# The last of 39 expert tiles added to the sums by one-hot matmuls in PSUM instead of by a scatter, and the final layer norm read from PSUM

## The reference

```
x = _layernorm(x + attn(x, ...), axis=-1)
x = _layernorm(x + xattn(x, ctx, ctx, W, b), axis=-1)
x = _layernorm(x + ffn(x, Wg, bg, W1, b1, W2, b2), axis=-1)      # the change is in this line

def ffn(x, Wg, bg, W1, b1, W2, b2):
    gate_probs = softmax(einsum('bsd,de->bse', x, Wg) + bg)
    topk_probs, topk_idx = top_k(gate_probs, 2)                   # 8 experts
    weights = one-hot of topk_idx, weighted with topk_probs / their sum
    h = gelu(einsum('bsd,edf->bsef', x, W1) + b1)                 # 1024 hidden features
    y = einsum('bsef,efd->bsed', h, W2) + b2
    return einsum('bsed,bse->bsd', y, weights)
```

## Time and profile before

| | |
|---|---|
| median of three runs | 708.63 us (707.63 to 709.84) |
| the profiled execution: span from its first to its last instruction | 704.8 us |
| the profiled execution: its own time | not listed apart from its span; the median of the runs stands 3.8 us above the span |
| TensorE busy | 610.6 us, 87% of the span |
| VectorE busy | 517.4 us, 73% |
| ScalarE busy | 397.3 us, 56% |
| GpSimd busy | 292.9 us, 42% |
| mean granted TensorE clock | 0.964 of full speed |

### The profile page before, as it was taken

How to read it: one execution, slowest core, us unless ns; L and a number is a source line. 1 busy time by engine, 2 the same in 40 slices (tenths; PEclk the granted TensorE clock), 3 DMA queues, 4 the chain that set the end, 5 groups by cost and what they waited for, 6 DMA issues and landing times.

```text
span 704.8 us, 22698 instructions
## 1 busy us (share of the span) xinstructions
PE 610.6 (87%) x8063; PEld 447.7 (64%) x8064; DVE 517.4 (73%) x1106; ACT 397.3 (56%) x847; POOL 292.9 (42%) x245
## 2 busy tenths in 40 slices
PE   2678989999999999999886797899999999999940
PEld 1456756676676667667564556678777777777720
DVE  5797898997786878677677986867666666666635
ACT  4335668767568484866778693554434444444414
POOL 3688574436264641543111012233444444444422
PEclk9789999999999999999999997999999999999985
DMA  8435253240322304304344045122222222222226
GB/s 276 151 103 151 78 166 91 63 121 6 111 69 72 82 1 119 110 21 118 106 121 136 1 119 180 19 32 46 47 47 45 45 45 45 44 45 39 43 40 223
DMA packets 39839, 59.45 MB, mean 84 GB/s; under 512 B 6768, under 2 KB 27504, under 8 KB 39632
## 3 DMA queue, kind: packets, MB, share of 16 engines
q1 hardware_dynamic: 32272, 48.12, 23.3%
q0 software_dynamic: 7488, 10.23, 8.9%
HBM read 34.08 MB, written 11.67 MB: 65 GB/s over the span
## 4 chain that ended last, share of the span: by engine, by line
PE 34%; DVE 11%; DMA 6%; ACT 4%; issue 4%; POOL 2%; ACTq 1%; SPq 1%; DVEq 1%; POOLq 0%
PE bank L1688 6%; PE bank L1690 3%; DVE mxc L1085 3%; DMA x_sb<-x_rows,slot_row 2%; PE scores L1678 2%; PE bank L1678 2%; PE scores L1680 2%; PE scores L1679 2%; PE bank L1292 2%; DMA acc_rows<-x,slot_row 2%; PE bank L1680 2%; PE bank L1679 2%; POOL acc_rows L627 1%; ACT probs L742 1%; PE scores L1343 1%
## 5 line engine op out<-in xcount | busy, mean ns | idle before, releaser
L742 ACT ACTIVATE probs<-scores 128x768 f32<-128x768 f32 (+1 forms) x128 | 114.3, 918 | 51.0 <-PE scores L1349 40.2
L627 POOL DMA_INDIRECT acc_rows<-x,slot_row x39 | 65.2, 1671 | 132.7 <-DVE x L1198 129.8
L1688 PE MATMUL bank<-w_sb,wp 128*128 x312 | 109.9, 380 | 1.9 <-DVE wp L1185 1.9
L1085 DVE TENSOR_REDUCE mxc<-scores 128x4 f32<-128x1024 f32 x64 | 76.5, 1217 | 20.4 <-PE scores L1363 19.8
L1690 PE MATMUL bank<-w_sb,wp 128*128 x312 | 85.1, 273 | 0.0
L813 ACT ACTIVATE probs<-scores,b_sb 128x128 f32<-128x128 f32 x160 | 45.5, 368 | 63.3 <-PE scores L1680 63.3
L813 ACT ACTIVATE probs<-bank,b_sb 128x128 f32<-128x128 f32 x152 | 43.4, 370 | 65.6 <-PE bank L1680 65.6
L1183 DVE CAST wp<-probs 128x512 f16<-128x512 f32 x78 | 36.1, 462 | 60.3 <-ACT probs L813 59.8
L1050 DVE TENSOR_REDUCE mx<-scores 128x6 f32<-128x768 f32 x64 | 59.8, 950 | 15.7 <-PE scores L1331 15.2
L1678 PE MATMUL scores<-xT,w_sb 128*128 128x128 f16 x320 | 61.2, 223 | 2.2 <-DVE xT L909 1.2
L1679 PE MATMUL scores<-xT,w_sb 128*128 128x128 f16 x320 | 61.2, 223 | 0.0
(11 more groups left out here) (267 smaller groups left out, 1712.1 us busy)
## 6 DMA issues: line engine op xcount, KB each, us to landing
w_sb<-w_sb SPq DMA_DIRECT2D x192, 64.0 KB, 2.4
wstage<-in_w_exp SPq DMA_DIRECT2D x16, 512.0 KB
w_sb<-in_w_exp SPq DMA_DIRECT2D x8, 512.0 KB, 5.3
wp<-in_w_exp SPq DMA_DIRECT2D x8, 512.0 KB, 4.2
x_sb<-in_x_by_feature SPq DMA_DIRECT2D x8, 256.0 KB, 3.5
ctx_raw<-in_ctx SPq DMA_DIRECT2D x8, 256.0 KB, 3.1
x_res<-in_x SPq DMA_DIRECT2D x8, 256.0 KB, 3.5
x_rows<-x SPq DMA_DIRECT2D x8, 256.0 KB, 3.1
```

The source lines that it names most:

```text
L627: nc.gpsimd.indirect_dma_start(out=acc_rows[:, :], out_offset=bass.IndirectOffsetOnAxis(ap=slot_row[:, n:n + 1], axis=0), in_=yb[n % 2], i ...
L742: nc.scalar.activation(probs[:, 2 * (k % 4):2 * (k % 4) + 2, 0:cols], ps_p[pair[u, k, b]][:, :, 0:cols], ACT.Exp, scale=(SELF_SCALE, CROSS ...
L1085: nc.vector.tensor_reduce(mxc[:, 2 * k:2 * k + 2, :], ps_p[pair[u, k, b]][:, :, :].rearrange("p h (a k) -> p h a k", a=2), axis=AX.X, op=A ...
L1688: mm(o[:, 0:2 * D], ah[:, u, f, :], weights(e, at, 2 * D), start=(f == 0), stop=(f == FC - 1), skip_group_check=True)
```

## The change

The last tile, 38, is no longer scattered to HBM. Instead:

- GpSimd builds, for each of the 16 row tiles, a one-hot matrix of 128 slots by 128 rows in fp16 (onehot_last): element (s, l) is 1 where slot s of tile 38 holds row l of that row tile. First own_lane = row + 1 - 128 * t for each slot and row tile, then lane + 1 == own_lane, 17 operations. They stand behind the scatter of tile 35.
- VectorE's weigh of tile 38 writes its result as two fp16 parts, y_high and y_low, in place of one fp32 one.
- TensorE adds, for each row tile t, onehot_last[t] times y_high and times y_low into sums[t], a half of a PSUM bank: 32 matmuls. Then it adds fin, the loaded sums, by an fp32 matmul with the identity, one for each row tile (16), group by group as they land, and counts pe_sum.
- SP's loads of the sums wait for the scatters of tiles 0 to 37 only.
- bn_stats and the scaling read sums[t] in PSUM; ScalarE writes into fin. last_shift is one operation in place of two. VectorE scales both row tiles of the last group, ScalarE the other 14.

The new buffers lie over the weights of expert 1. The groups of LAST lie in different banks.

```diff
+        own_lane = w_sb[:, EW2:EW2 + 2 * NT].bitcast(F32)
+        onehot_last = w_sb[:, EW2 + 2 * NT:EW2 + 2 * NT + TOK].rearrange("p (t l) -> p t l", l=P)
+        y_high, y_low = [w_sb[:, EW2 + 2 * NT + TOK + i * D:EW2 + 2 * NT + TOK + (i + 1) * D] for i in range(2)]
...
+        sums = [bank[i][:, a * D:(a + 1) * D] for i in (0, 1, 4, 5, 2, 3, 7, 6) for a in range(2)]
...
@@ sync
-            sp.wait_ge(sc_st, 16 * N_TILES)
+            sp.wait_ge(sc_st, 16 * (N_TILES - 1))
             for k, (t0, t1) in enumerate(LAST):
                 sp.dma_start(fin[:, t0:t1, :], acc_st_rows[:, t0:t1, :]).then_inc(f_ld[k], 16)
             for k, (t0, t1) in enumerate(LAST):
-                sp.wait_ge(a_f, k + 1)
-                if k == len(LAST) - 1:
+                if k < len(LAST) - 1:
+                    sp.wait_ge(a_f, k + 1)
+                else:
                     sp.wait_ge(v_f, 1)
@@ gpsimd
-            for n in range(N_TILES):
+            for n in range(N_TILES - 1):
...
                 scatter(n)
-            pool.wait_ge(sc_st, 16 * N_TILES)
+                if n == N_TILES - 4:
+                    nc.gpsimd.tensor_scalar(own_lane, tab[:, C_CNT:C_CNT + NT], -1.0, slot_t[0][:, N_TILES - 1:N_TILES],
+                                            ALU.mult, ALU.add).then_inc(p_own, 1)
+                    pool.wait_ge(p_own, 1)
+                    for t in range(NT):
+                        last = nc.gpsimd.tensor_scalar(onehot_last[:, t, :], tab[:, C_LANE:C_LANE + P], 1.0, own_lane[:, t:t + 1],
+                                                       ALU.add, ALU.is_equal)
+                    last.then_inc(p_last, 1)
@@ scalar
-            for k, (t0, t1) in enumerate(LAST):
+            for k, (t0, t1) in enumerate(LAST[:-1]):
                 act_e.wait_ge(v_nb, k + 1)
-                for t in range(t0, t1 - (k == len(LAST) - 1)):
-                    last = nc.scalar.activation(fin[:, t, :], fin[:, t, :], ACT.Identity, bias=fnb[:, t:t + 1], scale=frs[:, t:t + 1])
+                for t in range(t0, t1):
+                    last = nc.scalar.activation(fin[:, t, :], sums[t], ACT.Identity, bias=fnb[:, t:t + 1], scale=frs[:, t:t + 1])
@@ vector, weigh
+                if final:
+                    nc.vector.tensor_scalar(y_high, yb[u], slot_w[:, n:n + 1], None, ALU.mult).then_inc(v_last, 1)
+                    dve.wait_ge(v_last, 1)
+                    nc.vector.scalar_tensor_tensor(y_low, yb[u], slot_w[:, n:n + 1], y_high, ALU.mult, ALU.subtract).then_inc(v_last, 1)
+                else:
+                    nc.vector.tensor_scalar(yb[u], yb[u], slot_w[:, bass.ds(n, 1)], None, ALU.mult).then_inc(v_y, 1)
@@ vector, the end
-                link(nc.vector.tensor_tensor(fnb[:, at], fmv[:, at, 0], frs[:, at], ALU.mult))
-                nc.vector.tensor_scalar(fnb[:, at], fnb[:, at], -1.0, None, ALU.mult).then_inc(v_nb, 1)
+                nc.vector.scalar_tensor_tensor(fnb[:, at], fmv[:, at, 0], -1.0, frs[:, at], ALU.mult, ALU.mult).then_inc(v_nb, 1)
             for k, (t0, t1) in enumerate(LAST):
-                dve.wait_ge(f_ld[k], 16)
+                dve.wait_ge(pe_sum, k + 1)
                 for t in range(t0, t1):
-                    last = nc.vector.bn_stats(fst[:, t, :], fin[:, t, :])
+                    last = nc.vector.bn_stats(fst[:, t, :], sums[t])
...
-            last_shift(len(LAST) - 1)
-            t = NT - 1
-            nc.vector.tensor_scalar(fin[:, t, :], fin[:, t, :], fmv[:, t, 0:1], frs[:, t:t + 1], ALU.subtract, ALU.mult).then_inc(v_f, 1)
+            dve.wait_ge(p_rsf, len(LAST))
+            for t in range(*LAST[-1]):
+                last = nc.vector.tensor_scalar(fin[:, t, :], sums[t], fmv[:, t, 0:1], frs[:, t:t + 1], ALU.subtract, ALU.mult)
+            last.then_inc(v_f, 1)
@@ tensor
+            pe.wait_ge(v_y, N - 1)
+            pe.wait_ge(p_last, 1)
+            for i, y in enumerate((y_high, y_low)):
+                pe.wait_ge(v_last, i + 1)
+                for t in range(NT):
+                    mm(sums[t], onehot_last[:, t, :], y, start=(i == 0 and t % 2 == 0), stop=False, skip_group_check=True)
+            for k, (t0, t1) in enumerate(LAST):
+                pe.wait_ge(f_ld[k], 16)
+                for t in range(t0, t1):
+                    last = mm(sums[t], ident, fin[:, t, :], start=False, stop=True, skip_group_check=True)
+                last.then_inc(pe_sum, 1)
```

More of the change, by code:

```diff
@@ L421, in decoder_layer @@
         v_varf, p_rsf = sem("final_variance_ready"), sem("final_root_ready")
+        p_own, p_last, v_last, pe_sum = sem("last_lanes_known"), sem("last_onehots_ready"), sem("last_output_split"), sem("pe_sums")
         v_ch = sem("vector_chain")
@@ L1185, in split_hidden, with weigh @@
                 nc.vector.tensor_tensor(al[:, u, at, :], act[:, u, at, :], ah[:, u, at, :], ALU.subtract).then_inc(v_al, 1)
-            def weigh(n, u, after):
+            def weigh(n, u, after, final=False):
                 e = dve.value_load(tile_e[0:1, bass.ds(n, 1)], min_val=0, max_val=E - 1)
@@ L1197, in weigh @@
                 dve.wait_ge(v_yt, n * 2 + 2)
-                nc.vector.tensor_scalar(yb[u], yb[u], slot_w[:, bass.ds(n, 1)], None, ALU.mult).then_inc(v_y, 1)
+                if final:
[4 more added lines that the diff above has]
+                    nc.vector.tensor_scalar(yb[u], yb[u], slot_w[:, bass.ds(n, 1)], None, ALU.mult).then_inc(v_y, 1)
             def tile(n, u, following=True):
@@ L1239, in _ @@
             split_hidden(N_TILES - 1, 0, 1)
-            weigh(N_TILES - 1, 0, (N_TILES - 2) * 16)
+            weigh(N_TILES - 1, 0, (N_TILES - 2) * 16, True)
             def last_shift(k):
```

## The result

The changed kernel takes 712.8 us (median of 5 runs, 711.2 to 714.98) against 707.63 us for the kernel before in the same session (5 runs, 705.81 to 709.84): a ratio of 1.0079, 95% interval 1.0055 to 1.0103. It is slower by 5.2 us where 3 us less were forecast. The profiled execution of the changed kernel is the slowest of its five: 714.98 us, a span of 713.2 against 704.8.

The account below looks back on a forecast made before the run. The bound was a serial tail of 26 us: scatters, loads, VectorE's statistics, ScalarE's scaling. The terms gave 704.8 - 2.95 = 701.85 us of span, 708.63 - 2.95 = 705.7 us; 8-in-10 range 703.9 to 709.2.

Parts of the forecast that it names:

- The one-hots on GpSimd: Build between scatters 35 and 36: 0.27 us each, ending at 671.8, some 0.6 us late.
- supposed upper bound of 0.42: Highest price taken for one GpSimd one-hot, from a two-input tensor_tensor of 512 columns scaled to 128: 0.42 us.
- cover of 4.26 us: GpSimd's free time between scatters 35 and 36, from 667.21 to 671.47, taken to hide the one-hot build.
- signs named for a wrong forecast: One-hots over 0.3 us with scatter 36 past 672.5; clock 0.50 between 680 and 690; statistics awaiting TensorE, or over 0.40 us.
- The rival with a chance of 0.05: GpSimd one-hots over 0.6 us, comparison looping slower than a product; at 0.7 loads 7.5 us late, about 712 us; chance 0.05.
- The last scatter leaves the path: Before the loads of the sums: they wait for scatter 37 alone and start 4.55 us earlier if nothing delays it.
- y_low hidden: VectorE's extra output of tile 38 adds 0.42 us, hidden behind the first 16 matmuls, which need y_high only.
- 32 one-hot matmuls under the loads: TensorE, 0.11 us each at full clock, done at 683.4 before the first load at 683.8: no cost; uncovered 3.5 us.
- 16 identities: fp32 matmuls between each load and its statistics: 0.46 us a row tile, 2.0 us for a group of four, paid once.
- Statistics from PSUM, shift in one operation: VectorE's final stage: one 0.20 us operation fewer a group, 2.22 becomes 2.03 us; reading PSUM costs nothing.
- ScalarE from PSUM: ScalarE's last stretch: 8 tiles left, not 9, at 0.46 us each, between bounds 0.39 and 0.52; ends at 697.9.
- TensorE's clock falls for a while (0.2): Rival, chance 0.2: a 1.5 us pause before the one-hot matmuls halves the clock; up to 1.7 us lost, 707.4 us.

Follow-up runs that it names:

- before_build: The kernel before plus only the 17 GpSimd one-hot operations behind the scatter of tile 35, results unused: 716.76 us against 707.84, ratio 1.0124.
- half_build: The changed kernel with eight one-hots built early, one per tile from tile 20, eight left behind scatter 35: 708.46 us against 707.23 for the kernel before, ratio 1.0013.
- spread: The changed kernel with GpSimd's one-hots built one in each of tiles 20 to 35: 705.67 us against 707.84 for the kernel before, ratio 0.9972.
- psum_only: The changed kernel without one-hots: all 39 tiles scattered, loaded sums still passed through PSUM; 710.84 us against 707.84 for the kernel before, ratio 1.0043.
- spread_again: The same kernel as spread, rerun side by side with dve_again: 704.74 us against 708.8 for the kernel before, ratio 0.9954.
- spread_six: spread with the 16 row tiles of the last stage in six groups instead of five: 706.54 us against 707.23 for the kernel before, ratio 0.9981.
- dve_build: spread with the one-hots made by VectorE, eight in each of tiles 8 and 9: 701.45 us against 707.23 for the kernel before, ratio 0.9918.
- dve_again: The same kernel as dve_build, rerun side by side with spread_again: 705.54 us against 708.8 for the kernel before, ratio 0.9973.
- probe: spread plus unused GpSimd operations of several forms in tiles 12 to 18, run once; add and compare on 512 columns adds 0.93 us over 256.
- probe2: spread plus further unused GpSimd forms (copy, two inputs, other column counts) in tiles 12 to 18, run once; two inputs on 256 columns 0.93 us.

## Why the prediction was wrong

- **The one-hots on GpSimd** are the step that failed: "One input and a narrow output are nearer to the memset; I take 0.27." Measured is 0.80 us each (the small one takes 0.84, of which 0.34 behind the scatter's issue). The nearer row by the count of inputs said nothing of the form of the instruction, and the supposed upper bound of 0.42 lay below the one-hot and below even two inputs at this width (0.47 to 0.66). Scatter 37 followed scatter 35 9.1 us later than before where 0.6 was forecast. before_build shows this term alone (+8.9 us), half_build that it grows once the cover of 4.26 us is used up, and spread that it goes when the build is elsewhere. Two of the signs named for a wrong forecast came: one-hots over 0.3 us with scatter 36 at 683.05, past 672.5, and a clock of 0.51 from 685 on, which follows from the late scatters. Two side sums were off as well: at 0.42 the build would be 3.0 us late by the forecast's own numbers, not 2.8, and the 1.8 for 0.28 us a one-hot comes out as 0.7 without the fixed part of 0.10 and 2.3 with it.
- **The rival with a chance of 0.05** (over 0.6 us, at 0.7 loads 7.5 us late, about 712 us) had the place and nearly the price: 0.80, scatters 9.1 late, 712.8. Its reason, a comparison slower than a product, finds no support: a comparison alone (0.72) is faster than an addition alone (0.88); a product was not measured.
- **The last scatter leaves the path**: right. From scatter 37 to the loads 8.6 us became 3.9, forecast 4.55 less.
- **y_low hidden**: right. It starts at 688.38 for 0.48 us, beside the first matmuls.
- **32 one-hot matmuls under the loads**: right in cost, 0.11 each at full clock in spread, and nothing on the path, though the margin of 0.4 us wasn't there. In spread they start at 681.21 and end at 684.86, 0.4 us behind the first load's landing (684.4); the second load, for which TensorE waits 0.50 us, hides that. In the changed kernel they end before the first load even with the clock fallen.
- **16 identities**: right. A group of four is 2.0 us (1.13 and 0.88 in the chains), paid once.
- **Statistics from PSUM, shift in one operation**: right, 2.02 us a group for 2.03.
- **ScalarE from PSUM**: right, 0.46 forecast; three tiles in 1.48 and four in 1.83 us with their ends. The loads-to-end stretch was forecast at 701.85 - 681.1 = 20.75 and is 20.6 in spread, 21.3 in the changed kernel, where the second load landed 5.2 us behind the loads' start (the identities start at 697.09), not 4.87. In spread it landed after 4.5.
- **TensorE's clock falls for a while (0.2)**: not where it was feared. A pause of 1.56 us left the clock full (spread). The late scatter made the pause 7.40 us, and the clock did fall, but under the wait for the loads. Priced in psum_only it is 1.84 us. The forecast set the risk by the length of the pause, between 1.31 and 1.88 us; in the changed kernel the clock was still full 3.9 us into one, so these rows don't order by length alone.

Without the 0.6 us for the build the forecast's gain in the tail is 2.95 + 0.6 = 3.55 us. From scatter 35 to the end, the five profiles with an early build of all sixteen gain 2.4 to 4.2 us on before (39.18 us; 34.97 in spread, 35.41 in spread_again, 35.28 in spread_six, 36.74 in dve_build, 35.00 in dve_again). In the whole kernel spread has -2.2 and -4.1 us by medians in two sessions. That this is near -2.95 is partly luck: its longer tile loop, which the forecast did not have, takes 1.5 us back.

What stays open: why GpSimd's one-hots lengthen the tile loop, and why a tensor_scalar of one column takes 0.65 us when two follow each other.

## What to carry to other kernels

Price an operation that the trace doesn't show on an engine by its instruction form as well as its size, and when no row of that form exists, don't call a row of another form an upper bound. Put work that depends on nothing late in the program far ahead of the last serial chain, since it delays each scatter behind it in the same queue once its cover is used up (8.9 us in before_build). Which engine does it matters little once it is early: 0.22 us on VectorE against 0.80 or more on GpSimd, with no difference between the medians side by side. Matmuls that run while a load is awaited can be worth more than nothing: they keep the clock up for the ones on the path.

## What the runs showed of the hardware

- GpSimd's tensor_scalar from 128 fp32 columns to fp16 takes 0.72 to 0.88 us in each form tried (probe), a copy 0.42 (probe2), a two-input operation 0.47 to 0.66 (both).
- With one-hots on GpSimd in the tile loop VectorE's cast of 128x512 takes 487 to 494 ns in the mean, without them 446 to 463.
- TensorE's clock, full after a pause of 1.56 us (spread), fell within pauses of 7.40 us (after) and 9.51 us (psum_only), in both at about 685, some 4 to 4.5 us behind the last matmul. In before it was at 0.50 already from 341 on, behind a pause of 1.88 us; what makes the difference is not shown. In after it came back about 3.4 us behind the first matmul, in psum_only about 5 us behind it. The Trainium skill, "TensorE: Matmul & The Clock Gate" (section "What's actually happening"), has activity releasing the throttle; the rows agree.
- An execution reaches the same instruction, scatter 0, up to 6.8 us earlier or later with the same program ahead of it (448.45 to 455.23). A change of 3 us is read from a stage, or from many runs, not from two spans.
